# Position network's biases on VectorE, its steps placed anew, and products that nobody reads in a wait of the second layer

## The reference

```python
# layer 0: Fourier mixing and an MLP
x = L0(x)        # layernorm, 2D rfft, block-diagonal complex 12x12 mix + bias, relu, irfft, + x, MLP with gelu, + x
# layer 1: Toeplitz mixing
def rpe_forward(pos, pw, pb, lw, lb, ow, ob):          # the position network; 31 lags, 128 wide
    x = relu(pos @ pw + pb)
    for i in range(3):
        x = relu(srms(x)) @ lw[i] + lb[i]
    return relu(srms(x)) @ ow + ob
xn = srms(x)
u, v = silu(xn @ Wu + bu), silu(xn @ Wv + bv)
out = u * (toeplitz(v, a_h, rows) + toeplitz(v, a_w, columns))   # a_h, a_w: rpe_forward with r2_*, r1_*
x = out @ Wo + bo + x
# layers 2 and 3: layernorm, w_in, two bidirectional GRUs over 256 tokens, gates, w_out, + x
```

## Time and profile before

| | us |
|---|---|
| median of 3 runs | 1099.58 |
| the three runs | 1099.35, 1099.58, 1105.99 |
| the profiled execution | 1105.72 |
| its span, first to last instruction | 1103.8 |
| TensorE busy | 1014.7 |
| VectorE busy | 883.8 |
| ScalarE busy | 790.3 |
| mean granted TensorE clock | 0.562 |

### The profile page before, as it was taken

How to read it: one execution, slowest core, us unless ns; L and a number is a source line. 1 busy time by engine, 2 the same in 40 slices (tenths; PEclk the granted TensorE clock), 3 DMA queues, 4 the chain that set the end, 5 groups by cost and what they waited for, 6 DMA issues and landing times. The chain is left out here.

```text
span 1103.8 us, 55393 instructions
## 1 busy us (share of the span) xinstructions
PE 1014.7 (92%) x22230; PEld 847.7 (77%) x22230; DVE 883.8 (80%) x6019; ACT 790.3 (72%) x4622; POOL 32.3 (3%) x20
## 2 busy tenths in 40 slices
PE   4786798899999999999999898999999999999997
PEld 3563788588888888888888767888888888888886
DVE  7544346788888888999999867888888899999994
ACT  5323471777778878888888637788888788888882
POOL 1001140000000000000000000000000000000000
PEclk9586797755555555555555566555555555555555
DMA  4010410000000000000000000000000000000001
GB/s 133 2 17 13 114 33 1 7 4 4 4 4 4 4 4 5 4 4 4 4 4 4 3 6 4 4 4 4 4 5 4 4 4 4 4 4 4 4 4 30
DMA packets 14942, 13.03 MB, mean 12 GB/s; under 512 B 12370, under 2 KB 13843, under 8 KB 14396
## 3 DMA queue, kind: packets, MB, share of 16 engines
q1 hardware_dynamic: 14684, 9.49, 3.7%
HBM read 8.65 MB, written 0.83 MB: 9 GB/s over the span
## 5 line engine op out<-in xcount | busy, mean ns | idle before, releaser
L1260 PE MATMUL L2s_reset_sum<-L2s_h_hi,L_w_hidden 97*128 97x8 f16 x2048 | 139.7, 179 | 12.0 <-DVEq L1104 0.7
L1260 PE MATMUL L3s_reset_sum<-L3s_h_hi,L_w_hidden 97*128 97x8 f16 x2048 | 139.4, 179 | 11.9 <-DVEq L1104 0.4
L1127 DVE TENSOR_TENSOR_SCAN L3s_h_hi<-L3s_renew,L3s_terms 96x32 f16<-96x32 f32 x512 | 113.1, 221 | 43.6
L1127 DVE TENSOR_TENSOR_SCAN L2s_h_hi<-L2s_renew,L2s_terms 96x32 f16<-96x32 f32 x512 | 113.1, 221 | 43.5
L1260 PEld LDWEIGHTS L2s_reset_sum<-L2s_h_hi,L_w_hidden 97*128 97x128 f16 x2048 | 94.5, 107 | 62.5 <-DVE L2s_h_hi L1127 14.1
L1260 PEld LDWEIGHTS L3s_reset_sum<-L3s_h_hi,L_w_hidden 97*128 97x128 f16 x2048 | 94.2, 107 | 62.4 <-DVE L3s_h_hi L1127 14.1
L1204 ACT ACTIVATE L3s_terms<-L3s_cand 96x16 f32<-96x16 f32 x512 | 111.8, 218 | 33.1
L1204 ACT ACTIVATE L2s_terms<-L2s_cand 96x16 f32<-96x16 f32 x512 | 111.6, 218 | 33.1
L1260 PE MATMUL L2s_cand_sum<-L2s_h_hi,L_w_hidden 97*128 97x8 f16 x2048 | 131.4, 175 | 2.6
L1260 PE MATMUL L3s_cand_sum<-L3s_h_hi,L_w_hidden 97*128 97x8 f16 x2048 | 131.3, 175 | 2.5
L1260 PE MATMUL L2s_keep_sum<-L2s_h_hi,L_w_hidden 97*128 97x8 f16 x2048 | 130.0, 174 | 0.0
(11 more groups left out here) (255 smaller groups left out, 3252.5 us busy)
## 6 DMA issues: line engine op xcount, KB each, us to landing
L_wih_raw<-in_L_wih SPq DMA_DIRECT2D x2, 1152.0 KB, 11.3
lagged<-in_L_w SPq DMA_DIRECT2D x1, 1296.0 KB, 8.7
L_w_hidden_raw<-in_L_whh SPq DMA_DIRECT2D x2, 576.0 KB
stream<-in_x SPq DMA_DIRECT2D x2, 384.0 KB, 3.8
out<-stream SPq DMA_DIRECT2D x4, 192.0 KB, 2.1
l_idft<-in_idft SPq DMA_DIRECT2D x1, 400.0 KB
rpe_lw<-in_rpe_lw SPq DMA_DIRECT2D x1, 384.0 KB
lagged<-coefs SPq DMA_DIRECT2D x16, 24.0 KB, 2.2
```

Of the source, the lines that this page charges most:

```text
L1127: e.tensor_tensor_scan(flat(h_hi[g][0:C, x]), flat(renew[g][:, x]), flat(terms[g][:, x]), 0.0, ALU.mult, ALU.add).then_inc(hi_ready[g], 1)
L1260: return e.matmul(dst, weights.hidden[0:rows, wp, GATES * (2 * g + j) + gate, :], rhs, start=False, stop=False, skip_group_check=True)
```

## The change

The biases of layers 1 to 3 of the network are no longer products of ones on TensorE. They are loaded to all 31 partitions, and VectorE adds them where it copied the product from PSUM. `layer(0)` stands right behind the DFT and the last evacuation; `normalise(0)` stands between VectorE's first and second part of the spread, its turned copy between the second and the third. Turns move from the sixth frequency of a bank to the eighth. In the tail of `toeplitz`, two products of 96x512 are written, once ahead of bank 0 and once ahead of bank 2, into the bank that the output then overwrites; nobody reads them.

```diff
                         e.tensor_scalar(share(spread, part)[:, :, :, n, :], share(spectrum, part), mask[:, n:n + 1], None,
                                         ALU.mult).then_inc(spread_ready, 1)
+                    if part == 0:
+                        rpe.normalise(e, 0)
+                    if part == 1:
+                        rpe.turned_copy(e, 0)
...
-                    if k <= DEPTH:
+                    if 1 <= k <= DEPTH:
                         rpe.normalise(e, k)
                         rpe.turned_copy(e, k)
...
                     last.then_inc(transformed, 1)
+                e.wait_ge(evacuated, BATCH)
+                rpe.layer(e, 0)
                 e.wait_ge(w_ready, 6)
...
-                    if f8 == 0 and k <= DEPTH:
+                    if f8 == 0 and 1 <= k <= DEPTH:
                         rpe.layer(e, k)
-                    if f8 == 5 and k <= DEPTH:
+                    if f8 == 7 and k <= DEPTH:
                         rpe.turn(e, k)
...
-        for dst, name in ((self.pos, "pos"), (self.rows, "rpe_rows"), (self.lw, "rpe_lw"), (self.ow, "rpe_ow"), (self.ob, "rpe_ob")):
+        for dst, name in ((self.pos, "pos"), (self.lw, "rpe_lw"), (self.ow, "rpe_ow"), (self.ob, "rpe_ob")):
             e.dma_start(dst[:], d[name]).then_inc(self.loaded, 16)
+        e.dma_start(self.rows[:], d["rpe_rows"][:, :, 0:2]).then_inc(self.loaded, 16)
+        e.dma_start(self.biases[:].rearrange("p a i f -> p a (i f)"),
+                    bass.AP(rows.tensor, 2 * RPE, [[0, LAGS], [a_stride, 2], [1, DEPTH * RPE]])).then_inc(self.biases_loaded, 16)
...
             else:
                 e.matmul(self.layer_bank[:, a, :], self.y_turned[:, a, :], self.lw[:, a, (i - 1) * RPE:i * RPE],
-                         start=True, stop=False)
-            e.matmul(self.layer_bank[:, a, :], self.ones[:], self.rows[:, a, 1 + i, :], start=False, stop=True)\
-                .then_inc(self.product, 1)
+                         start=True, stop=True).then_inc(self.product, 1)
...
-            self.link(e, e.tensor_copy(x[:], self.layer_bank))
+            if i == 1:
+                e.wait_ge(self.biases_loaded, 16)
+            self.link(e, e.tensor_tensor(x[:], self.layer_bank, self.biases[:, :, i - 1, :], ALU.add))
...
                 for k in range(NB):
                     half = k // 2
+                    if k % 2 == 0:
+                        e.wait_ge(gated, 3 * half + 1)
+                        for _ in range(2):
+                            e.matmul(bank(OUT + k)[0:C, :], w_u[:, 0:C], xT[0:C, 0:BANK], start=True, stop=True)
                     e.wait_ge(gated, 4 * (half + 1))
```

More of the change, by code:

```diff
@@ L507, in __init__ @@
         self.ones = sb("ones", [1, LAGS])
-        self.rows = sb("rows", [1, 2, 2 + DEPTH, RPE])
+        self.rows = sb("rows", [1, 2, 2, RPE])
+        self.biases = sb("biases", [LAGS, 2, DEPTH, RPE])
         self.lw = sb("lw", [RPE, 2, DEPTH * RPE])
@@ L525, in __init__ @@
         self.finished = sem("finished")
+        self.biases_loaded = sem("biases_loaded")
         self.links = 0
     def load(self, e, d):
-        for dst, name in ((self.pos, "pos"), (self.rows, "rpe_rows"), (self.lw, "rpe_lw"), (self.ow, "rpe_ow"), (self.ob, "rpe_ob")):
+        for dst, name in ((self.pos, "pos"), (self.lw, "rpe_lw"), (self.ow, "rpe_ow"), (self.ob, "rpe_ob")):
             e.dma_start(dst[:], d[name]).then_inc(self.loaded, 16)
+        e.dma_start(self.rows[:], d["rpe_rows"][:, :, 0:2]).then_inc(self.loaded, 16)
+        rows = d["rpe_rows"]
+        a_stride = (2 + DEPTH) * RPE
+        e.dma_start(self.biases[:].rearrange("p a i f -> p a (i f)"),
+                    bass.AP(rows.tensor, 2 * RPE, [[0, LAGS], [a_stride, 2], [1, DEPTH * RPE]])).then_inc(self.biases_loaded, 16)
     def layer(self, e, i):
@@ L543, in layer @@
                 e.matmul(self.layer_bank[:, a, :], self.pos[:], self.rows[:, a, 0, :], start=True, stop=False)
+                e.matmul(self.layer_bank[:, a, :], self.ones[:], self.rows[:, a, 1, :], start=False, stop=True)\
+                    .then_inc(self.product, 1)
             else:
                 e.matmul(self.layer_bank[:, a, :], self.y_turned[:, a, :], self.lw[:, a, (i - 1) * RPE:i * RPE],
-                         start=True, stop=False)
-            e.matmul(self.layer_bank[:, a, :], self.ones[:], self.rows[:, a, 1 + i, :], start=False, stop=True)\
-                .then_inc(self.product, 1)
+                         start=True, stop=True).then_inc(self.product, 1)
     def turn(self, e, i):
```

## The result

The changed kernel's median is **1093.9 us** over seven runs (1089.59 to 1094.52), beside 1105.87 for the kernel before over seven (1099.35 to 1106.13). The ratio is 0.9901, with a 95% interval of 0.9876 to 0.9927: 1.0% faster. The time itself was forecast (1093.8), but not the ratio of 0.995, because the three runs of before that were known had a median of 1099.58. So it has two usual times, 7 us apart, and a median of a few runs lands on the one or the other.

What follows compares the result with a forecast made beforehand. Recurrences were taken as nine tenths of the span; the mixing stage as bound by the TensorE-VectorE chain. 1105.72 - 6.4 (chain) - 4.8 (tail) = 1094.5, or 1099.58 - 6.4 = 1093.2 for quick executions; forecast 1093.8 us, own range 1091.5 to 1096.

Steps and rivals of the forecast that it cites:

- Chain, the start: First layer's mixing stage, position network: earlier layer 0 and split spreads end normalise(1) at 36.3, not 38.74: 2.4 us gained.
- Chain, the rounds: Position network's TensorE-VectorE rounds: 6.0 us each instead of 7.60, 1.6 less, for two rounds, with VectorE late next.
- Chain, the end: After y(3), the last normalising: four frequencies instead of six ahead of the output products, 0.85 us less.
- The bias addition: VectorE's addition in place of the 0.41 us copy from PSUM: 0 to 0.13 us extra each, taken as 0, three times.
- Tail: Second layer's output products: unread products fill the 2.47 us pause and keep the clock full, 4.8 us gained.
- The second pair: Unread products ahead of bank 2: end at 183.8, about when VectorE's second-half gating ends (183.48); no gain assigned.
- The next stage: 0: First products of the stage behind the tail: gain between 0 and 1.9 us, taken as 0 because VectorE's rows come no earlier.
- 1099.58 - 6.4: Quick executions, supposed to keep the tail's clock already: unread products win and cost nothing, only the 6.4 us remains, giving 1093.2.
- (1): Rival: both savings also for the median, 1099.58 - 11.2 = 1088.4; sign: median 11 us below before; chance 0.2.
- (2): Rival: tail clock falls all the same, second unread pair costs 3.7 us: 1103.0; sign: half clock behind the pause; chance 0.1.
- (3): Rival: mixing-stage chain gives half, 3 us in place of 6.4: 1096.5; sign: ReLU beginning after 55; chance 0.12.
- (4): Rival: the tail's pause is harmless, the half clock has another cause, unread products win nothing: 1099.3; chance 0.05.

Runs made afterwards that it cites:

- the places alone: Changed kernel with biases again as products of ones and a copy, and no unread products: 1095.65 us, ratio 0.9926 against the kernel before.
- both edits in one kernel: Changed kernel with layer three's second weight products ahead of the first turns, plus unread products around the MLP's norm: 1092.83 us, ratio 0.9892.
- the turn at the sixth: Changed kernel with the turn back at the sixth frequency of a bank instead of the eighth: 1094.97 us, ratio 0.9919.
- the bridge: Changed kernel with one more unread product of 96x512 behind the last output bank: 1093.12 us, ratio 0.9917.
- the second trace of before: The kernel before, unchanged, profiled once more for a trace of its quick group: one execution, 1098.76 us.
- the chain: As a run: the changed kernel without the unread products in the second layer's tail: 1094.06 us, ratio 0.9931 against the kernel before.
- the biases alone: The kernel before with only the biases moved to VectorE, old places, no unread products: 1099.43 us, ratio 0.9962.
- the one with one pair: Changed kernel with only the first pair of unread products, none ahead of bank 2: 1092.8 us, ratio 0.9902.

## Why the prediction was right, and where it was not

The time was right, partly by errors that offset each other. By its own steps:

**Chain, the start** (2.4 us forecast): y(1) was over at 35.71, not 36.3, so 3.0. Right mechanism, the term 0.6 too small: the last part of the spread was over at 28.46 + 2.72 = 31.18, not 31.5, and the next round took over from the mixing sooner than counted (below).

**Chain, the rounds** (1.6 us each forecast): 5.73 instead of 7.60, so 1.87 each. VectorE is late next, as forecast; but the mixing hands over 37.90 - 36.54 = 1.36 us behind the layer's start, not 1.6, because the next instruction on VectorE starts 1.06 us after the mixing's start and does not wait for all of its 1.19. Two rounds: 0.5 us.

**Chain, the end** (0.85 forecast): y(3) was over at 47.19, and the last mixing started 3.50 us behind it, where 5.26 lay before: 1.76. Two frequencies fewer are worth the 0.85; over the rest the clock was full from 45.10 to 48.30, which nothing had foreseen and which shortens that stretch. The other traces show it: with two frequencies fewer and the clock at half, this stretch takes 4.42 us (the places alone) and 4.41 (both edits in one kernel), which is 5.26 - 0.85; with all the frequencies back and half a clock it takes 5.27 (the turn at the sixth), and with the clock full until about 49.7 it takes 2.93 (the bridge). The remaining 0.9 us are the clock, and not every execution has them.

Together 8.5 in place of 6.4, above the upper bound of 7 (8.0 against the second trace of before). The parts run singly fit: the places take 0.85 us out of a round (6.75, the expected figure), the turn's place alone 0.86 (6.59 against 5.73), the biases 1.0, where 0.7 was expected. The bias addition costs what the copy did, 0.40 against 0.41: the bottom of its range, as taken.

**Tail** (4.8 forecast): 4.88 against the first trace. That the unread products shorten it is shown from both sides: the same products added to before shorten the tail to 5.65, taken out of after they give 9.07. But 10.52 was the unusual value. Five other traces without the full set of products have 8.98 to 9.19, so that the term's usual worth is 3.4 us: the clock stays full for another 1.5 us behind the pause and falls then. That 4.8 was met is luck of the trace it was read from. In the time the tail's gain is smaller still, since the stages behind give back 1.7 us in the traces, and the medians with and without the unread products are the same.

**The second pair** was forecast to lie hidden behind the gating, and no gain was put to it. It is hidden, but it is the pair on which the gain hangs: it holds the clock over its own pause of 1.47 us, and without it the tail is 8.98 us long.

**The next stage: 0** (between 0 and a gain of 1.9): wrong, it is a loss of 1.39 us here. The bound excluded a loss without a reason. With the clock kept, the first weight products are done in 1.93 to 2.66 us, not 3.70; VectorE's rows are not earlier, so TensorE waits 0.71 to 1.45 us, and the second group runs at half clock (3.17 us, where 1.88 is the full-clock figure). Before, the stage began at half and the clock was full for that group; after, it began at full, fell inside the first group, ahead of the wait, and was back only for the third group. The inner wait is thus not what ended the full clock in after. Filled with work it left the fall where it was and brought the clock back 3.4 us sooner, and the stage took 16.70 us in two traces of three (18.07 in the third, where the clock fell ahead of the stage); bridging the pause ahead of the stage moved the fall and not the return. What makes the clock fall in the first group is open.

**The two groups of before**: wrong. The quick executions do not keep the tail's clock; they have it back sooner in the MLP and value stages. So "1099.58 - 6.4", for which the tail was to win nothing, rested on a false premise. Against the second trace of before, after's span is 7.5 us shorter: the chain 8.0 and the tail 3.4 us gained, 0.7 ahead of the MLP's norm, less 2.8 in the MLP, where only the quick execution had the full clock, and less 1.9 in all stages behind the tail. That 1093.2 came out near is thus two gains larger than I counted (by 1.6 and 3.4), against losses that I did not count; and of the 2.6 us by which after's median lies above its profiled execution there is no trace.

**The rivals.** (1), both savings at full size from 1099.58, is 1088.4; only one of seven runs comes near (1089.59), and the give-back is part of the reason. The median did fall 12 us between the two series, but by the group on which the median of before lies. So the sign that the prediction named for this rival, a median 11 us lower, appeared without the rival's cause; it was no sign that could tell. (2), the clock falls all the same: no, 1.00 up to 178.05. (3), half a chain: no. (4), the pause is harmless: no. Behind pauses of 2.47 us the clock fell at once in one trace and 1.5 to 1.7 us later in four, and at the end of a pause of 1.47 us in one; behind pauses of 0.75 us in the same place it did not fall. The Trainium skill (TensorE: Matmul & The Clock Gate, the section on why this matters for your kernels) allows pauses of up to about 3 us; the traces of five kernels here speak against that (the kernel before, the chain, the places and the biases alone, and the one with one pair). One rival reading is not excluded: the unread products differ from the output products around them not only in filling a pause, they are also of 512 columns, where those are bound by weight loads. The output products lost a full clock in the midst of gapless work (four traces) and did not regain it in 13.6 us; so it may be the kind of work, and not the filled pause, that holds the clock, though 49 products of that kind ran at a full clock for 5.5 us in the MLP. No run puts light products into the pause, or 512-column products where there is none.

**A misreading without consequence**: the recurrences of layers three and four are four fifths of the span (two of 437 and 438 us in 1103.8), not nine tenths, and the clock is not at half throughout: two slices between them stand at 0.6.

**Open** is why an execution of the same instructions has its clock back ahead of the MLP's products and another only in the midst of them, and so which of the two times comes. No run shows what decides it, and the medians of after, of the one with one pair and of the one with the bridge cannot be told apart.

## What to carry to other kernels

Where one wait separates two bursts of TensorE work, read the granted clock on both sides of it; a couple of unread products there can shorten the burst behind it by more than they cost (3.4 us here), and half of that can be lost again in the next stage; look at the whole time before keeping them. Real work moved into such a wait shortened its stage by 2 us in two traces of three. Whatever is made faster ahead of a wait for a producer that is not faster lengthens that wait, so cost the stage behind a clock gain as a possible loss. Before a forecast leans on a difference between single runs, take a trace of each kind: the same kernel can have two usual times, and a median of three can lie in the less frequent one. Where both kernels have such groups, compare group with group as well as the medians.

## What the runs showed of the hardware

- The same program, unchanged, took 1098.76 and 1105.72 us, and the difference lies in three stretches in which the clock was full in one and half in the other: the ten MLP products took 4.56 us where it was back ahead of them, and 7.83 where it was not.
- A pause need not be the moment of the fall: behind 2.47 us without products the clock was 0.50 at once in the first trace, and 1.00 for 1.5 us more in the second (172.30 to 173.80).
- The clock rose for about 3 us amid small single-precision products and waits (from 45.10 in after, from 36.40 in the biases' kernel), while 3.57 us of gapless half-precision products of 512 columns, followed by single-precision ones, left it at 0.50 up to 629.20.
- Products bound by weight loads ran at a full clock for up to 3.8 us behind two unread products (32 in 3.81 and in 3.73 us) and for 5.5 us in the MLP (49 records), lost it 1.5 to 1.7 us into gapless work in four traces without them, and did not raise it in 13.8 us at 0.50.
